# A two-layer chain of convolution and low-rank feed-forward: 7-product form one pair earlier, weight sums on GpSimd

## The chip, the core and the metric

The kernel runs on one core of a Trainium2 chip. A core has TensorE (PE in the profile; matmuls, which it writes to PSUM banks of 128 x 512 numbers), VectorE (DVE), ScalarE (ACT), GpSimd (POOL), and the queues that start DMA transfers (here those of SyncE, SP, and of ScalarE). Each engine works through its own list of instructions in order and waits on semaphores for the others. The metric is the device time of one launch in microseconds.

## What is computed

Two layers, each of them a mixing step over channels and a feed-forward step with low-rank experts, on x of 32 x 64 x 1024 numbers in float32:

```python
# layer 0: grouped convolution (9 taps, 4 groups) plus a row made from cond_128
h = conv(x, L0_cond_weight) + (c @ c_weight.T)[:, :, None] + bias[None, :, None]
out = h @ W.T + b                               # 1024 x 1024
scores = h @ gate_w.T + gate_b                  # 4 ranks, the best one is taken
final = (h @ A[:r].T @ B[:, :r].T) * weight     # r of the chosen rank, 8 to 64
x = x + out + final
# layer 1: per-sample 64 x 64 channel mix, then the same with 8 experts of rank 16
h = einsum('boi,bih->boh', agg_w, x) + agg_b[:, :, None]
out = h @ W_base.T + b_base
weights = sparsemax(h @ W_router.T)
x = x + out + einsum('bser,bse,ero->bso', einsum('bsd,edr->bser', h, A1), weights, B1)
```

## The kernel before, in words

**Tiles and pairs.** 2048 rows make 16 tiles of 128 rows a layer. Two tiles make a pair; pairs 0 to 7 are layer 0, pairs 8 to 15 layer 1. For each pair TensorE makes the mixed input of the *next* pair (`conv_half`, `mix_half`; tiles t1+2 and t2+2) between the matmuls of this pair, VectorE adds the row to it (`sum_mix`, into `mixed`), and the result is split into a high part and a rest (`split_a`: ScalarE copies to `a_hi` in a reduced format, VectorE subtracts to get `a_lo`). A product of two matrices then takes three matmuls: high x high, high x rest, rest x high. Weights are split the same way.

**Two ways to multiply.** `FULL` pairs go by `dense0`: eight blocks of 128 of the contraction, and for each of them 3 output parts x 3 matmuls. The pairs after them go by a Strassen-like form: the two tiles of a pair and the two halves of the contraction are four operands A11, A12, A21, A22 and the 432 left and right output columns are the halves of the result, so that seven products P1 to P7 (`product_a`, `product_s`) take the place of eight. The columns that are left (`PLAIN`) go by `plain`. The seven-product form needs four sums of weight blocks, called T1 to T4, and four sums of input blocks, S1 to S4.

- T sums, layer 0: `t_sums(kc)` for kc = 0 to 3, four subtractions of 128 x 432 each, in place in `w_raw`; they make T1, T3, T2, T4 in that order. `split_t(i, kc)` splits them: ScalarE into `wb_hi`, VectorE into `wb_lo`. T3 lies in the slot of the weight block B12, so its split waits for the last matmul that reads B12 (`b12_read`).
- S sums: four operations of 128 x 512 on `mixed`. GpSimd makes them (`sums(g)`) for all pairs but the first that needs them; there VectorE does (`first_sums`). `split_s` splits them; `s_hi` and `s_lo` lie on the memory of `w_raw`.

**The gate.** For each tile `gate0(T)` reads the product's extra columns from the bank b_p, on VectorE: a chain of short instructions with one exponential on ScalarE in its middle (`gate_exp`), then four writes to `u_sb`, each to both halves of its columns. TensorE transposes `u_sb` into the bank `b_u` (`turn_u`), and `split_ut` splits the result into `ut_hi` and `ut_lo`. `lora` and `rank0` multiply these by the low-rank weights and add them to the results in the banks.

**Order.** It is written out by hand in each engine's list. Before the loop over g, the lists hold pair 0 and pair 1 in full (on TensorE: `dense0` of tile 0, `second_tile(0)`, `dense0` of tile 2, `second_tile(1)`). The loop runs from g = FULL to 15: `plain` of both tiles, P1, half a mix, transpose of tile t1, P2, half a mix, transpose of t2, P4, P5, `lora` of t1, half a mix, P6, half a mix, `lora` of t2, P7, P3, `lora`. VectorE's list in the loop: gate of t1, splits of S2 and S4, gate of t2, and then `take_first`, the sums of the mix, `split_ut`, `split_a`, and the additions to the rows `xs` in turn. Where TensorE waits for others in it is in the `wait_ge` lines: P4 waits for `tlo_done[T4]`, P5 for S1 and for `sum_mix(2g+2, 1)` (both write or read the bank b_y), `lora` for `utlo_done`, `plain` of tile t2 for `finq[1]`, the last addition of the pair before it.

**Where GpSimd stands.** After its constants it waits for the splits of T2 and T4, clears `kernels_sb`, and from then on makes S sums and, in pairs 3 to 6, the T sums of layer 1 (`prep`).

## Time and profile before

| | |
|---|---|
| three runs | 505.94, 506.79 (median), 506.85 us |
| the profiled execution | 505.61 us |
| its span, first to last instruction | 503.9 us |
| TensorE's granted clock over the span | 1.00 of 2.4 GHz |
| busy: TensorE, VectorE, ScalarE, GpSimd | 499.1, 347.9, 130.4, 142.0 us |

All times of the trace count from the start of the span. Idle time of an engine is written behind its row in square brackets, with what ended it. An instruction of VectorE begins a little before the one ahead of it has ended, so the distance of two starts is shorter than a duration.

### The profile page before, as it was taken

What the parts mean: (1) busy time and instruction counts of PE and PEld (TensorE: products, weight loads), DVE (VectorE), ACT (ScalarE), POOL (GpSimd) and SP (SyncE); (2) the same over time, 40 slices, a digit from 0 to 9 for tenths busy, and PEclk for the clock granted to TensorE, in tenths of its full rate; (3) what the DMA queues carried; (4) which work ended last, traced back from release to release, by engine and by line L of the source; (5) the groups of instructions that cost most, each with busy time, mean ns of one, the idle gap of its engine ahead of it and who ended that gap; (6) DMA issues with size and microseconds to landing.
All of it is one profiled execution on the core that took longest, in us unless ns stands there. A gap on an engine that the chain in (4) does not pass through costs nothing.

```text
span 503.9 us, 8309 instructions
## 1 busy us (share of the span) xinstructions
PE 499.1 (99%) x2981; PEld 467.7 (93%) x2981; DVE 347.9 (69%) x824; ACT 130.4 (26%) x272; POOL 142.0 (28%) x122
## 2 busy tenths in 40 slices
PE   8999999999999999999999999999999999999997
PEld 8999999999999999999999899999999999999986
DVE  3966988857766685776897975665747566574753
ACT  4732334212233122331252321210212111111200
POOL 1000010003443142431205462441516244152620
PEclk9999999999999999999999999999999999999999
DMA  8845204428476574657899752433425233340212
GB/s 317 320 144 166 91 1 148 157 89 262 163 245 195 196 231 171 197 184 268 273 410 339 298 168 87 145 102 126 130 69 161 85 129 103 134 138 19 103 47 84
DMA packets 41125, 84.34 MB, mean 167 GB/s; under 512 B 3803, under 2 KB 24667, under 8 KB 41084
## 3 DMA queue, kind: packets, MB, share of 16 engines
q1 hardware_dynamic: 31884, 61.16, 36.6%
q10 hardware_dynamic: 9200, 22.65, 12.3%
q8 instruction: 24, 0.39, 0.3%
q14 instruction: 17, 0.14, 0.1%
HBM read 58.82 MB, written 24.97 MB: 166 GB/s over the span
## 4 chain that ended last, share of the span: by engine, by line
PE 98%; DMA 1%; DVE 1%; issue 0%; ACT 0%; DVEq 0%
PE b_p L1265 10%; PE b_x L1283 7%; PE b_x L1286 7%; PE b_x L1285 7%; PE b_m L1231 6%; PE b_p L1266 5%; PE b_y L1285 5%; PE b_y L1286 5%; PE b_y L1283 5%; PE b_m L1241 3%; PE b_w L1283 2%; PE b_z L1285 2%; PE b_w L1285 2%; PE b_z L1286 2%; PE b_z L1283 2%; PE b_w L1286 2%
## 5 line engine op out<-in xcount | busy, mean ns | idle before, releaser
L566 ACT CAST a_hi<-mixed 128x512 fp32r<-128x512 f32 x63 | 38.1, 620 | 167.4 <-DVE mixed L870 88.3
L1265 PE MATMUL b_p<-wp,a_hi 128*128 128x464 f32 (+1 forms) x224 | 72.5, 377 | 0.0
L512 POOL TENSOR_TENSOR xs<-xs,mixw_sb 128x464 f32<-128x464 f32 (+1 forms) x28 | 36.3, 1307 | 115.2 <-DMA xs<-x_scratch 81.5
L1266 PE MATMUL b_p<-wp,a_lo 128*128 128x232 f32 (+1 forms) x224 | 60.0, 268 | 0.0
L882 DVE TENSOR_TENSOR s_lo<-mixed,s_hi 128x512 fp32r<-128x512 f32 x56 | 45.4, 834 | 20.5 <-ACT s_hi L578 20.5
L578 ACT CAST s_hi<-mixed 128x512 fp32r<-128x512 f32 x56 | 34.7, 621 | 77.3 <-POOL mixed L484 41.2
L875 DVE TENSOR_TENSOR a_lo<-mixed,a_hi 128x512 fp32r<-128x512 f32 x63 | 47.4, 779 | 9.4 <-ACT a_hi L566 8.8
L484 POOL TENSOR_TENSOR mixed<-mixed 128x512 f32<-128x512 f32 x13 | 17.6, 1353 | 120.9 <-DVE a_lo L875 120.9
L976 DVE TENSOR_TENSOR xs<-b_x,xs 128x464 f32<-128x464 f32 (+1 forms) x54 | 33.5, 620 | 22.9 <-PE b_x L1286 20.0
L1265 PEld LDWEIGHTS b_p<-wp,a_hi 128*128 128x128 f32 x224 | 42.0, 188 | 4.7
L1266 PEld LDWEIGHTS b_p<-wp,a_lo 128*128 128x128 f32 x224 | 42.7, 191 | 0.2
L1283 PE MATMUL b_y<-wb_hi,s_hi 128*128 128x464 f32 (+1 forms) x112 | 41.2, 368 | 0.0
L1285 PE MATMUL b_y<-wb_lo,s_hi 128*128 128x464 f32 (+1 forms) x112 | 41.1, 367 | 0.0
L1286 PE MATMUL b_y<-wb_hi,s_lo 128*128 128x464 f32 (+1 forms) x112 | 41.1, 367 | 0.0
L1231 PE MATMUL b_m<-first_in,blk 128*128 128x128 f32 x256 | 32.0, 278 | 0.2 <-DMA blk<-in_xblk 0.2
L976 DVE TENSOR_TENSOR xs<-b_y,xs 128x432 f32<-128x432 f32 (+1 forms) x28 | 17.4, 620 | 20.8 <-PE b_y L1286 20.0
L1231 PEld LDWEIGHTS b_m<-first_in,blk 128*128 128x128 f32 x256 | 30.8, 194 | 0.7 <-DMA blk<-in_xblk 0.5
L1283 PE MATMUL b_x<-wb_hi,s_hi 128*128 128x432 f32 (+1 forms) x80 | 30.5, 381 | 0.0
L1286 PE MATMUL b_x<-wb_hi,s_lo 128*128 128x432 f32 (+1 forms) x80 | 29.2, 365 | 0.0
L1285 PE MATMUL b_x<-wb_lo,s_hi 128*128 128x432 f32 (+1 forms) x80 | 29.2, 365 | 0.0
L1283 PEld LDWEIGHTS b_y<-wb_hi,s_hi 128*128 128x128 f32 x112 | 21.0, 188 | 2.0
L1286 PEld LDWEIGHTS b_y<-wb_hi,s_lo 128*128 128x128 f32 x112 | 21.0, 188 | 1.9
(260 smaller groups left out, 1210.0 us busy)
## 6 DMA issues: line engine op xcount, KB each, us to landing
blk<-x_scratch SPq DMA_DIRECT2D x16, 512.0 KB, 3.3
blk<-in_xblk SPq DMA_DIRECT2D x14, 516.0 KB, 3.9
xs<-in_x SPq DMA_DIRECT2D x16, 296.0 KB, 3.6
x_scratch<-xs SPq DMA_DIRECT2D x16, 296.0 KB, 4.5
w_raw<-in_wcat SPq DMA_DIRECT2D x8, 546.0 KB, 8.3
xs<-x_scratch SPq DMA_DIRECT2D x14, 280.0 KB, 3.2
out_dram<-xs SPq DMA_DIRECT2D x14, 280.0 KB, 2.5
praw<-in_wcat ACTq DMA_DIRECT2D x8, 464.0 KB, 6.1
```

The source lines that it names most:

```text
L512: pool.tensor_tensor(x_rows, x_rows, bbase[:, a:b], ALU.add).then_inc(x_biased[q], 1)
L566: act.copy(a_hi[:, op, :, :], mixed[:, op, :, :]).then_inc(ahi_done[op], 1)
L578: act.copy(s_hi[:, i, :, :], mixed[:, S_AT[i], :, :]).then_inc(shi_done[i], 1)
L875: dve.tensor_tensor(a_lo[:, op, :, :], mixed[:, op, :, :], hi(a_hi[:, op, :, :]), ALU.subtract).then_inc(alo_done[op], 1)
L882: dve.tensor_tensor(s_lo[:, i, :, :], mixed[:, S_AT[i], :, :], hi(s_hi[:, i, :, :]), ALU.subtract).then_inc(slo_done[i], 1)
L976: dve.tensor_tensor(x_rows, src[:, 0:HALF[l]], x_rows, ALU.add).then_inc(done, 1)
L1231: ins = pe.matmul(dst, blk[s][:, at + side:at + side + QB], taps, start=(side == 0), stop=(side == 1))
L1265: pe.matmul(both, x_hi, wp[:, k, :, 0:PLAIN[l]], start=(k == 0), stop=False, skip_group_check=True)
L1266: ins = pe.matmul(dst, x_lo, wp_hi[:, k, 0:PLAIN[l]], start=False, stop=(k == NCH - 1), skip_group_check=True)
L1283: pe.matmul(dst, x_hi[:, k, :], w_hi[:, k, :], start=(first and k == 0), stop=False, skip_group_check=not first)
L1285: pe.matmul(dst, x_hi[:, k, :], w_lo[:, k, :], start=False, stop=False, skip_group_check=not first)
L1286: ins = pe.matmul(dst, x_lo[:, k, :], w_hi[:, k, :], start=False, stop=(k == HK - 1), skip_group_check=not first)
```

## The change

- `FULL` is 1: pair 1 (tiles 2 and 3) goes by the seven products. Its entries in the lists ahead of the loop are gone, and the loop begins at g = 1.
- The T sums (16 subtractions) are made by GpSimd, not by VectorE, once `a_lo` of A22 of pair 0 is made; behind them GpSimd makes the S sums of pair 1 (`sums(FULL)`), which makes `first_sums` of VectorE disappear.
- The 32 splits of T (16 on ScalarE, 16 on VectorE) stand in other places: those of T1, T4 and half of T2 within pair 0, those of T3 and the rest of T2 in pair 1.
- For tiles 2 to 15 (`together`), the gate writes its result once, for the two tiles of a pair side by side, and one transpose turns both (`turn_pair`, behind the second half mix); `split_ut` then works on 64 partitions of the bank instead of 128.

```diff
-FULL = 2
+FULL = 1
...
+        def together(T):
+            return 2 * FULL <= T < TILES
...
+            pool.wait_ge(alo_done[A22], 1)
+            for kc in range(HK):
+                t_sums(kc)
+            sums(FULL)
...
-                    for t in (T1, T2, T3, T4):
+                    for t in (T1, T3):
                         act.wait_ge(tlo_done[t], HK)
...
+                if together(T):
+                    rows_ = turned_rows(s)
+                    act.copy(ut_hi[rows_, s, :], b_u[rows_, 0:P]).then_inc(uthi_done, 1)
+                    act.copy(ut_lo[0:RANK, s, :], b_u[rows_, 0:P]).then_inc(uthi_second, 1)
+                    return
...
@@ vector, pair 0 @@
+            split_t(T1, 0)
+            split_t(T4, 0)
             dve.wait_ge(att_t, 1)
...
             finish(0, 0)
+            split_t(T1, 1)
             dve.wait_ge(aggb_mm, 1)
             dve.tensor_copy(aggb_sb[:, :], b_m[0:NB, 2 * P:2 * P + CH]).then_inc(aggb_copied, 1)
+            split_t(T4, 1)
+            split_t(T2, 0)
+            split_t(T2, 1)
             gate0(1)
             sum_mix(2, 0)
+            split_t(T1, 2)
             sum_mix(2, 1)
+            split_t(T4, 2)
             split_a(A11, 1)
...
             finish(1, 0)
-            t_sums(0)
-            t_sums(1)
...
@@ vector, loop @@
+                if g == FULL:
+                    split_t(T1, 3)
+                    split_t(T4, 3)
                 gate(2 * g + 1)
                 if g == FULL:
-                    split_ut(2 * g)
-                    for i in S_ORDER:
+                    for kc in range(HK):
+                        split_t(T3, kc)
+                    for i in (S2, S4, S1):
                         split_s(i, g)
...
+                if together(2 * g):
+                    split_ut(2 * g)
                 split_ut(2 * g + 1)
+                if g == FULL:
+                    split_t(T2, 2)
+                    split_t(T2, 3)
+                    split_s(S3, g)
...
@@ tensor @@
-            pe.wait_ge(sum_done, 7)
-            pe.wait_ge(finq[0], 1)
-            for k in range(NCH):
-                dense0(2, k)
-            pe.wait_ge(sum_done, 8)
-            second_tile(1)
...
-                turn_u(t1)
+                if not together(t1):
+                    turn_u(t1)
...
-                    turn_u(t2)
+                    if together(t1):
+                        turn_pair(g)
+                    else:
+                        turn_u(t2)
```

Three places in the lists. VectorE in pair 0, from the addition of the left columns of tile 0 (`xs0<-b_p0`) to the first instructions of the gate of tile 1, before:

```order
L991 TENSOR_TENSOR xs0<-b_p0,xs0 128x160
L1088 COPY aggb_sb<-b_m 32x64
L921 TENSOR_TENSOR sc<-b_p1,first_in 128x4
L922 SCALAR_TENSOR_TENSOR pm<-sc 128x4
L923 TENSOR_SCALAR st<-pm 128x1
```

and in the changed kernel (`wb_lo<-w_raw,wb_hi` is a split of a T sum):

```order
L1015 TENSOR_TENSOR xs0<-b_p0,xs0 128x160
L830 TENSOR_TENSOR wb_lo<-w_raw,wb_hi 128x432
L1115 COPY aggb_sb<-b_m 32x64
L830 TENSOR_TENSOR wb_lo<-w_raw,wb_hi 128x432 x3
L941 TENSOR_TENSOR sc<-b_p1,first_in 128x4
L942 SCALAR_TENSOR_TENSOR pm<-sc 128x4
L943 TENSOR_SCALAR st<-pm 128x1
```

Four splits have moved ahead of the gate of tile 1.

GpSimd from its last constant on, before:

```order
L477 MEMSET ut_lo 1x256
L517 MEMSET kernels_sb 128x2048
L484 TENSOR_TENSOR mixed<-mixed 128x512
L487 TENSOR_TENSOR mixed<-mixed 128x512
```

and in the changed kernel, the last of four equal groups of T sums and what follows:

```order
L525 TENSOR_TENSOR w_raw<-w_raw 128x432
L526 TENSOR_TENSOR w_raw<-w_raw 128x432
L528 TENSOR_TENSOR w_raw<-w_raw 128x432
L530 TENSOR_TENSOR w_raw<-w_raw 128x432
L492 TENSOR_TENSOR mixed<-mixed 128x512
L495 TENSOR_TENSOR mixed<-mixed 128x512
L497 TENSOR_TENSOR mixed<-mixed 128x512
L500 TENSOR_TENSOR mixed<-mixed 128x512
L539 MEMSET kernels_sb 128x2048
```

Sixteen T sums and four S sums now stand ahead of the clearing of `kernels_sb`.

VectorE in the changed kernel, pair 1, from the end of the gate of tile 3 to the second half of the next mix (in the list before, pair 2 had one `ut_hi` row, four `s_lo`, `xs0` and the two sums here):

```order
L953 TENSOR_SCALAR u_sb<-hid_sb,kw 128x32
L830 TENSOR_TENSOR wb_lo<-w_raw,wb_hi 128x432 x4
L895 TENSOR_TENSOR s_lo<-mixed,s_hi 128x512 x3
L1000 TENSOR_TENSOR xs0<-b_x,xs0 128x432
L880 TENSOR_TENSOR mixed<-b_m,ctx_row 128x8x64
L880 TENSOR_TENSOR mixed<-b_y,ctx_row 128x8x64
L888 TENSOR_TENSOR a_lo<-mixed,a_hi 128x512 x2
L905 TENSOR_TENSOR ut_hi<-b_u,ut_hi 64x128 x2
```

The four splits of T3 stand ahead of the splits of S, and both `ut_hi` rows of the pair behind `a_lo`.

## Rows read from the trace of the kernel before

**Rows 1.** The page: engines; chain that ended last; a ScalarE group.
```profile
PE 499.1 (99%) x2981; PEld 467.7 (93%) x2981; DVE 347.9 (69%) x824; ACT 130.4 (26%) x272; POOL 142.0 (28%) x122
...
PE 98%; DMA 1%; DVE 1%; issue 0%; ACT 0%; DVEq 0%
...
L578 ACT CAST s_hi<-mixed 128x512 fp32r<-128x512 f32 x56 | 34.7, 621 | 77.3 <-POOL mixed L484 41.2
```
**Rows 2.** Timeline of TensorE (start, duration, what): starts of pairs 1 to 4, P5.
```profile
48.56 0.31 PE L1364 MATMUL b_p<-wp,a_hi 128*128 128x228 f32 x1
...
82.13 0.41 PE L1265 MATMUL b_p<-wp,a_hi 128*128 128x456 f32 x1
...
114.97 0.37 PE L1265 MATMUL b_p<-wp,a_hi 128*128 128x456 f32 x1
...
130.89 0.36 PE L1283 MATMUL b_y<-wb_hi,s_hi 128*128 128x432 f32 x1
...
145.98 0.37 PE L1265 MATMUL b_p<-wp,a_hi 128*128 128x456 f32 x1
```
**Rows 3.** Timeline of GpSimd, then of VectorE, around the start of pair 3.
```profile
113.83 1.29 POOL L487 TENSOR_TENSOR mixed<-mixed 128x512 f32<-128x512 f32 x1
115.19 1.62 POOL L489 TENSOR_TENSOR mixed<-mixed 128x512 f32<-128x512 f32 x1
116.96 1.56 POOL L492 TENSOR_TENSOR mixed<-mixed 128x512 f32<-128x512 f32 x1
...
114.37 1.29 DVE L882 TENSOR_TENSOR s_lo<-mixed,s_hi 128x512 fp32r<-128x512 f32 x1 [1.61 <-ACT s_hi L578]
...
118.05 0.49 DVE L921 TENSOR_TENSOR sc<-hid_sb,first_in 128x4 f32<-128x4 f32 x1
```
**Rows 4.** The same two engines within pair 3.
```profile
129.90 1.20 POOL L502 TENSOR_TENSOR praw<-praw 128x464 f32<-128x464 f32 x1
131.18 1.53 POOL L504 TENSOR_TENSOR praw<-praw 128x464 f32<-128x464 f32 x1
...
130.11 3.13 DVE L875 TENSOR_TENSOR a_lo<-mixed,a_hi 128x512 fp32r<-128x512 f32 x2 [0.69 <-ACT a_hi L566]
```
**Rows 5.** Timeline of VectorE: pair 0, and four splits of T3.
```profile
23.37 1.27 DVE L875 TENSOR_TENSOR a_lo<-mixed,a_hi 128x512 fp32r<-128x512 f32 x2
...
36.09 0.61 DVE L976 TENSOR_TENSOR xs<-b_x,xs 128x432 f32<-128x432 f32 x1 [0.67 <-PE b_x L1313]
...
38.44 0.21 DVE L1088 COPY aggb_sb<-b_m 32x64 f32<-32x64 f32 x1 [1.00 <-PE b_m L1431]
39.76 0.16 DVE L921 TENSOR_TENSOR sc<-b_p,first_in 128x4 f32<-128x4 f32 x1 [1.10 <-PE b_p L1376]
...
42.33 0.68 DVE L867 TENSOR_TENSOR mixed<-b_m,ctx_row 128x512 f32<-128x512 f32 x1
43.83 0.69 DVE L867 TENSOR_TENSOR mixed<-b_x,ctx_row 128x512 f32<-128x512 f32 x1 [0.81 <-PE b_x L1231]
...
47.13 0.29 DVE L890 TENSOR_TENSOR ut_hi<-b_u,ut_hi 64x128 fp32r<-64x128 f32 x1
...
51.13 0.32 DVE L991 TENSOR_TENSOR xs<-b_p,xs 128x160 f32<-128x160 f32 x1
...
69.45 2.17 DVE L798 TENSOR_TENSOR wb_lo<-w_raw,wb_hi 128x432 fp32r<-128x432 f32 x4
```
**Rows 6.** Timeline of TensorE: first low-rank matmul of tiles 0, 1 and 6.
```profile
35.49 0.36 PE L1311 MATMUL b_x<-lb,ut_hi 128*128 128x432 f32 x1
...
47.48 0.46 PE L1311 MATMUL b_z<-lb,ut_hi 128*128 128x432 f32 x1
...
133.25 0.36 PE L1311 MATMUL b_z<-lb,ut_hi 128*128 128x432 f32 x1
```
**Rows 7.** Timeline of TensorE: half a convolution early and later.
```profile
4.61 2.46 PE L1231 MATMUL b_m<-first_in,blk 128*128 128x128 f32 x16 [0.20 <-DMA blk<-in_xblk]
...
45.42 1.95 PE L1231 MATMUL b_m<-first_in,blk 128*128 128x128 f32 x16
```

More of the change, by code:

```diff
@@ L694, in _ @@
             split_ut(1)
+            act.wait_ge(b12_read, 1)
+            split_t(T3, 0)
+            split_t(T3, 1)
             split_a(A21, 1)
             split_a(A22, 1)
-            for kc in (0, 1):
-                for i in (T1, T2, T4):
-                    split_t(i, kc)
-            gate_exp(2)
-            for kc in (2, 3):
-                for i in (T1, T2, T4):
-                    split_t(i, kc)
-            split_ut(2)
-            act.wait_ge(b12_read, 1)
-            for kc in range(HK):
-                split_t(T3, kc)
-            gate_exp(3)
-            split_a(A11, 2)
-            split_a(A12, 2)
-            split_ut(3)
-            split_a(A21, 2)
-            split_a(A22, 2)
-            for i in S_ORDER:
-                split_s(i, FULL)
+            split_t(T1, 3)
+            split_t(T4, 3)
             for g in range(FULL, LAST + 1):
@@ L721, in _ @@
                 gate_exp(2 * g)
+                if g == FULL:
+                    split_t(T3, 2)
+                    split_t(T3, 3)
                 if g > FULL:
@@ L739, in _ @@
                     load_slot(T3, P7)
-                split_ut(2 * g)
+                if g == FULL:
+                    split_t(T2, 2)
+                    split_t(T2, 3)
+                    for i in (S2, S4, S1, S3):
+                        split_s(i, g)
+                if not together(2 * g):
+                    split_ut(2 * g)
                 if g < LAST:
@@ L751, in _ @@
                     split_a(A12, g + 1)
+                if together(2 * g):
+                    split_ut(2 * g)
                 split_ut(2 * g + 1)
@@ L888, in split_ut @@
                 dve.wait_ge(uthi_done, T + 1)
-                if T < TILES:
+                if together(T):
+                    rows_ = turned_rows(s)
+                    dve.wait_ge(uthi_second, T + 1)
+                    dve.tensor_tensor(ut_hi[turned_rows(1 - s), s, :], b_u[rows_, 0:P], hi(ut_hi[rows_, s, :]),
+                                      ALU.subtract).then_inc(utlo_done, 1)
+                elif T < TILES:
                     dve.tensor_tensor(ut_hi[RANK:P, s, :], src[RANK:P, :], hi(ut_hi[RANK:P, s, :]),
@@ L918, in gate0 @@
                 hid = hidden(T)
-                if T > 1:
+                if together(T):
+                    dve.wait_ge(ut_done, T - s)
+                elif T > 1:
                     dve.wait_ge(ut_done, T - 1)
@@ L1099, in _ @@
             finish(1, 0)
-            t_sums(0)
-            t_sums(1)
-            for i in (T1, T2, T4):
-                split_t(i, 0)
-            t_sums(2)
-            for i in (T1, T2, T4):
-                split_t(i, 1)
-            gate0(2)
-            t_sums(3)
-            for kc in (2, 3):
-                for i in (T1, T2, T4):
-                    split_t(i, kc)
-            split_ut(2)
-            for kc in range(HK):
-                split_t(T3, kc)
-            finish(0, 1)
-            gate0(3)
-            sum_mix(4, 0)
-            sum_mix(4, 1)
-            split_a(A11, 2)
-            split_a(A12, 2)
-            split_ut(3)
-            sum_mix(5, 0)
-            sum_mix(5, 1)
-            take_plain(1, 1)
-            finish_first(1, 1)
-            split_a(A21, 2)
-            split_a(A22, 2)
-            first_sums()
-            finish_second(1, 1)
             def take_first(g):
@@ L1140, in _ @@
                     split_s(S4, g)
+                if g == FULL:
+                    split_t(T1, 3)
+                    split_t(T4, 3)
                 gate(2 * g + 1)
                 if g == FULL:
-                    split_ut(2 * g)
-                    for i in S_ORDER:
+                    for kc in range(HK):
+                        split_t(T3, kc)
+                    for i in (S2, S4, S1):
                         split_s(i, g)
@@ L1147, in _ @@
                     take_first(g)
-                if g == PAIRS - 1:
-                    split_ut(2 * g)
                 if g < LAST:
                     sum_mix(2 * g + 2, 0)
-                if g not in (FULL, PAIRS - 1):
+                if not together(2 * g):
                     split_ut(2 * g)
@@ L1161, in _ @@
                     split_a(A12, g + 1)
+                if together(2 * g):
+                    split_ut(2 * g)
                 split_ut(2 * g + 1)
+                if g == FULL:
+                    split_t(T2, 2)
+                    split_t(T2, 3)
+                    split_s(S3, g)
                 if PREP_FIRST <= g <= PREP_LAST:
```

47 lines of the change are left out of this document (30 added, 17 removed).

## Prediction

> **What bounds the kernel now.** I read three views: the page (engines and chain), TensorE's timeline at the borders of the pairs, and the timelines of VectorE and GpSimd side by side. TensorE is busy 499.1 us of a span of 503.9 and makes up 98% of the chain that ended last [rows 1]. So work taken from TensorE comes straight off the time, as long as its operands are there when it comes to them; work on the others costs nothing until it makes TensorE wait. TensorE's timeline gives the price of a pair: pair 1, in full, lasts from 48.56 to 82.13, 33.57 us; pair 3, by seven products, from 114.97 to 145.98, 31.01 us [rows 2]. (Pair 2 holds other work too and is no measure.) The question is then whether VectorE, ScalarE and GpSimd deliver what pair 1 needs 34 us earlier than now.
>
> **Taken from TensorE.** Pair 1 by seven products: 33.57 - 31.01 = 2.56 us. One transpose less in each of seven pairs: it is 128 columns wide like one of the 16 steps of half a convolution, which take 1.95 us, some 0.11 each [rows 7]; since TensorE overlaps neighbours I take half of that, 0.05 us each, between 0 and 0.11: 0.35 us. Together 2.9 us.
>
> **What GpSimd and VectorE do to each other.** This decides the case. At 114.37 VectorE begins a subtraction of 128x512 from two operands in SBUF while GpSimd is in a sum that ends at 113.83 + 1.29 = 115.12. It ends at 115.66, that is 0.54 us after GpSimd's end, with 1.29 us in place of the 0.64 of an undisturbed one, two of which take 1.27 [rows 3, 5]. GpSimd's next sum takes 1.62 in place of 1.29. So the one who comes second stands still until the other's instruction is over. In pair 3 the same gives two subtractions in 3.13 us [rows 4], against 1.27 undisturbed [rows 5]: 1.5 to 1.6 us each while GpSimd has a queue of sums. Even an instruction of 4 columns waits: it takes 0.49 us at 118.05 and ends with GpSimd's sum at 118.52 [rows 3]; the like one with one operand in PSUM at 39.76 takes 0.16 [rows 5]. Additions that read one operand from PSUM aren't hit.
>
> GpSimd now makes 16 sums of 128x432. None is in the trace; the 128x464 one takes 1.20 [rows 4], so 1.20 x 432/464 = 1.12 each, 18 us in all. It starts where `a_lo` of A22 ends, at 23.37 + 1.27 = 24.6 [rows 5]; alone it would be busy to 42.6, and with VectorE's instructions of about 0.4 to 0.5 between them to about 47. Over just this stretch VectorE has its new splits, each with two SBUF operands: each costs 1.12 + some 0.37 = 1.5 us instead of the 0.52 of rows 5 (four in 2.17).
>
> **Pair 0, step by step.** (a) From 24.6 to 36 VectorE has eight such instructions (two in the gate of tile 0, two that split the low-rank weights, two new splits, two that make the attention diagonal). Its idle stretches there take up the first ones. I estimate that the two new splits end near 35.7 and `ut_hi` at 36.0, where TensorE wants it at 35.49 [rows 6]: 0.5 late. The diagonals wait about 1.1 each, so the addition that starts at 36.09 starts at about 38.1. (b) The addition's group lasts to about 39.5. Then four splits at 1.5 us, 5.9: the gate of tile 1 starts at 45.3 and not at 39.76. The idle 1.00 + 1.10 us there [rows 5] would have covered four undisturbed splits to the tenth of a us; it doesn't cover 5.9. (c) The gate has two more instructions with two SBUF operands; they wait once for about 1.0: 6.4 late at the next row, 42.33. (d) Two more splits, 0.52 each if GpSimd is done by then, one of them in the idle 0.81 before 43.83 [rows 5] and the other in a wait for ScalarE: 0.4 comes back. The split `ut_hi` of tile 1 (47.13) is the last thing before TensorE's 47.48, with no slack there [rows 5, 6]. So pair 1 starts about 5.9 us late; TensorE has waited for it in the pieces that end at the low-rank matmul of tile 0, the copy of `aggb_sb`, the transpose of tile 1, the bank b_m and the low-rank matmul of tile 1. Bounds: with the part before 38 at nothing and no wait in the gate, 37.45 + 6.1 gives 3.8 late, less 0.3: 3.5. With sums of 1.25 us, each step longer: 7.7.
>
> **Pair 1.** All times here are those before plus 5.9. (e) `plain` of tile 3 wants the addition at 51.13 + 0.32 = 51.45 finished; it is due 2.55 after the pair's start, at 51.11 [rows 2, 5]. Before, nothing there waited for it. 0.35 us; between 0.2 and 0.5. (f) P5 is due 130.89 - 114.97 = 15.92 after the start of a pair [rows 2], so at 48.56 + 5.9 + 0.35 + 15.9 = 70.7. It waits for `sum_mix(4, 1)`. VectorE's list up to it: gate of tile 2 from 57.4, 2.57 us (39.76 to 42.33) [rows 5] plus 0.3 for the reduction ahead of it, plus about 2.2 for two waits, since GpSimd's four S sums (1.29 each and more) [rows 3] run from 56.1 to 61.7: 62.5. Two splits, 1.1: 63.6. Gate of tile 3, 2.9: 66.5. Four splits of T3, 2.1: 68.6. ScalarE may make `s_hi` only after these, 0.62 [rows 1]; then three `s_lo` of 0.61, `xs` 0.55, two sums of the mix 0.65 each: 72.9. P5 waits 2.2 us. Between 0.8 (no wait in the gate of tile 2) and 2.9. P4, and the transpose of the pair, are due at 68.3 and have what they need. P6 and P7 need T2, S3 by 75 and later: no wait.
>
> **Later pairs.** (g) `split_ut` of the first tile has moved behind `a_lo`. In pair 3, `a_lo` ends at 130.11 + 3.13 = 133.24 and TensorE wants `ut_hi` at 133.25 [rows 4, 6]: 0.3 us late, in this pair alone, since GpSimd's sums came later there than in pairs 4 to 6. Otherwise nothing: the S sums of pair 2 on GpSimd have the place that they have in pair 3 now. The removed `first_sums` and 16 T sums shorten VectorE's list by some 11 us, all of it beside TensorE's work, worth nothing.
>
> **Sum.** 5.9 + 0.35 + 2.2 + 0.3 - 2.9 = +5.8 us on a span of 503.9: 509.7, and with the 1.7 us around it 511.4. The profiled execution (505.61) lies 1.2 below the median of the runs; on the median, 506.79 + 5.8 = **512.6 us**, slower by 1.1%. Ends of the terms: 3.5 + 0.2 + 0.8 - 2.9 = +1.6 and 7.7 + 0.5 + 2.9 + 0.3 - 2.9 = +8.5, so 508.4 to 515.3.
>
> **Rivals.** *Faster:* the two engines don't hold each other up here, or GpSimd's sums find gaps between VectorE's instructions. Then (b) leaves 0.4 late, (e) 0.35, (f) nothing: 0.75 + 0.3 - 2.9 = -1.9, 504.9 us. For it: the four splits then fit the idle 2.1 us; against it: rows 3 and 4, with the same kind of instruction. It decides when a split in pair 0 takes under about 0.9 us. *Short instructions slip through:* full-size ones wait, those of the gate don't. Then the gate terms of (c) and (f) and part of (a) go: some 3.5 late in pair 0, 0.8 at P5: 508.5 us. Against it: the row at 118.05. The Trainium skill ("SBUF — State Buffer", section "Who interferes with whom") says that issue order, not an instruction's shape, decides who blocks; by that this rival is out, and the trace agrees with the 0.49 us of a 4-column row. *Slower still:* TensorE waits some 6 us in pieces within 22 us, and its granted clock, 1.00 throughout now, may fall from 2.4 to 1.2 GHz for a while. At the start half a convolution takes 2.46 us against 1.95 [rows 7], part of it at the lower level; if 3 us of work ran at that level, they would take 6: 515.6 us. The Trainium skill ("TensorE: Matmul & The Clock Gate", section "What's actually happening") has an idle TensorE fall back to the lower level; the trace has no wait long enough to show it. That the change doesn't do what it says can be excluded: the lists show the seven products of pair 1.
>
> **How the numbers follow.** Forecast 512.6 with 0.63; clock 0.06; short instructions slip through 0.12; faster 0.13; and 0.06 for a mixture of small waits that ends near zero. The range leaves out the faster case and half of the last: 507.5 to 516.5. A measurement of this kernel tells about 0.2%, 1 us, from no change. Faster by more than that 0.13, within it 0.06, slower 0.81.
>
> **What would show it.** In the profile of the changed kernel: GpSimd busy from 24.6 to about 47 with 16 sums, many of 1.4 to 1.6 us; splits of T by VectorE of 1.5 us each between 39 and 46; idle TensorE before the transpose of tile 1 and its low-rank matmul, about 4.5 us together, released by VectorE; pair 1 beginning near 54.5 and lasting 33.5 us, with 2 us of wait before P5; pairs 2 and later each shorter by 0.05. I am wrong if the splits there take 0.6, if the gate's 4-column instructions stay at 0.16, or if TensorE's waits are all under 0.5.

## The result, and the profile after

The changed kernel takes 515.15 us (median of six executions, 512.92 to 519.69) where the kernel before, measured beside it, takes 506.58 (505.48 to 508.54): a ratio of 1.0195, 95% interval 1.0168 to 1.0221. It is slower, by 8.6 us between the medians and by 9.4 us between the profiled executions (515.03 and 505.61). The forecast was 512.6, +5.8 us.

The page of the changed kernel: its engines, and the chain that ended last.

```profile
PE 501.0 (98%) x2946; PEld 467.3 (91%) x2946; DVE 353.3 (69%) x816; ACT 133.0 (26%) x276; POOL 174.7 (34%) x146
...
PE 82%; DVE 8%; DMA 5%; issue 1%; ACT 1%; ACTq 0%; SPq 0%; DVEq 0%
```

Against [rows 1], TensorE makes 35 matmuls fewer and is yet 1.9 us longer busy, GpSimd has 32.7 us more, and of the chain 8% is now VectorE and 5% DMA, which had 1% each. The waits of TensorE in the same profile (line waited for, releaser, us in total, times, longest) give the places:

```profile
PE b_m L1424 <- DVE att_rep L1083: 2.2, 1, 2.2
PE b_y L1293 <- DVE mixed L880: 2.2, 1, 2.2
PE b_z L1328 <- DVE ut_hi L908: 2.0, 1, 2.0
```

They are the attention's transpose, P5 of pair 1, and the low-rank matmul of tile 1. TensorE's timeline (start, duration, what, idle before it) shows what they do to the stages, to be held against [rows 2, 6]:

```profile
36.44 0.21 PE L1424 MATMUL b_m<-ident,att_rep 32*128 32x32 f32 x1 [2.24 <-DVE att_rep L1083]
...
39.10 0.56 PE L1328 MATMUL b_x<-lb,ut_hi 128*128 128x432 f32 x1
...
54.56 0.46 PE L1328 MATMUL b_z<-lb,ut_hi 128*128 128x432 f32 x1 [1.97 <-DVE ut_hi L908]
...
55.64 0.41 PE L1275 MATMUL b_p<-wp,a_hi 128*128 128x456 f32 x1
...
74.26 0.44 PE L1293 MATMUL b_y<-wb_hi,s_hi 128*128 128x432 f32 x1 [2.19 <-DVE mixed L880]
...
90.96 0.37 PE L1275 MATMUL b_p<-wp,a_hi 128*128 128x456 f32 x1
```

Pair 1 starts at 55.64 instead of 48.56, 7.1 us late. Of this, 0.5 us was there before any sum: the first product begins at 11.76 instead of 11.27, because the first half convolution, which runs partly at the lower level of the clock, took 2.98 us instead of 2.46 [rows 7]. It took 2.05 to 3.33 us in the profiled executions of this study, so this is no price of the sums. Pair 1 lasts 35.32 us instead of 33.57. At pair 2 the kernel is 8.8 us behind (90.96 against 82.13), and of the 9.4 us only 0.6 come later: pairs 2 to 6 take 157.0 us where they took 156.9, pair 7 27.8 against 27.4, pair 8 30.2 against 30.1.

Part of the 35.32 is the clock. These stretches of TensorE (from:to, length, busy and instructions, granted clock, DMA share, GB/s) lie at and behind the first two waits:

```profile
34.00:37.20 3.20, 0.96 (x7) 1.00 0.62 196
37.20:40.70 3.50, 3.50 (x14) 0.51 0.36 128
40.70:44.20 3.50, 3.50 (x23) 1.00 0.40 152
71.00:74.80 3.80, 1.61 (x9) 1.00 0.33 127
74.80:78.30 3.50, 3.50 (x12) 0.51 0.00 0
```

After standing still for 2.2 us TensorE resumed, and a moment later was granted 1.2 GHz in place of 2.4 for some 3.4 us, twice. Behind the third wait, 1.97 us, the level stayed at 1.00. The 12 matmuls of P5 took 3.99 us, from the start of the first to that of the next step (74.26 to 78.25), most of it at the lower level, against 2.36 in pair 4, so the second fall cost 1.6 us. The forecast sum had nothing for it.

What VectorE did in the gate of tile 0 and behind it (same columns):

```profile
25.76 0.66 DVE L942 TENSOR_TENSOR_SCAN pm<-sc 128x4 f32<-128x4 f32 x1
26.46 0.15 DVE L943 TENSOR_SCALAR st<-pm 128x1 f32<-128x1 f32 x1
26.53 0.98 DVE L944 TENSOR_SCALAR keep<-pm 128x3 f32<-128x3 f32 x1
...
27.94 0.75 DVE L948 TENSOR_TENSOR st<-st 128x1 f32<-128x1 f32 x1
28.73 1.16 DVE L949 TENSOR_SCALAR kw<-keep,st 128x4 f32<-128x4 f32 x1
29.92 0.73 DVE L956 TENSOR_SCALAR u_sb<-b_p,kw 128x16 f32<-128x16 f32 x4
...
35.28 1.02 DVE L1083 TENSOR_SCALAR att_rep<-att,stat 32x128 f32<-32x128 f32 x1
...
40.06 0.61 DVE L1000 TENSOR_TENSOR xs<-b_x,xs 128x432 f32<-128x432 f32 x1 [0.47 <-PE b_x L1330]
...
42.91 3.69 DVE L830 TENSOR_TENSOR wb_lo<-w_raw,wb_hi 128x432 fp32r<-128x432 f32 x3
46.52 0.15 DVE L941 TENSOR_TENSOR sc<-b_p,first_in 128x4 f32<-128x4 f32 x1
...
49.80 0.68 DVE L880 TENSOR_TENSOR mixed<-b_m,ctx_row 128x512 f32<-128x512 f32 x1
...
60.21 1.27 DVE L944 TENSOR_SCALAR keep<-pm 128x3 f32<-128x3 f32 x1
```

and three of GpSimd's sums, the first, a long one of the sixteen, and the first of the S sums:

```profile
25.29 1.12 POOL L525 TENSOR_TENSOR w_raw<-w_raw 128x432 f32<-128x432 f32 x1 [21.79 <-DVE a_lo L888]
...
30.89 2.12 POOL L526 TENSOR_TENSOR w_raw<-w_raw 128x432 f32<-128x432 f32 x1
...
57.35 1.29 POOL L492 TENSOR_TENSOR mixed<-mixed 128x512 f32<-128x512 f32 x1 [9.80 <-DVE a_lo L888]
```

Instructions of one to four columns take 0.66 to 1.27 us; alone, they take 0.16 to 0.23. They end with GpSimd's sums: the scan at 26.42, `keep` at 27.51, `st` at 28.69 and `kw` at 29.89, where the first four sums end at 26.41, 27.48, 28.67 and 29.86. In between, rows of one column with one operand (0.15) and rows that read PSUM went through. It goes both ways: the sum of 2.12 us began while VectorE was in a subtraction with two operands in SBUF and ended 1.0 us after that one.

### The profile page after: what moved, and what is told of

The parts are those of the page before. It is cut to its first block, busy times and chain, and to the rows that moved or that the text cites. A ratio compares the mean times of both kernels' runs of the same rounds, so it can differ in the third digit from the quotient of the medians.

```text
span 513.3 us, 8290 instructions
## 1 busy us (share of the span) xinstructions
PE 501.0 (98%) x2946; PEld 467.3 (91%) x2946; DVE 353.3 (69%) x816; ACT 133.0 (26%) x276; POOL 174.7 (34%) x146
## 4 chain that ended last, share of the span: by engine, by line
PE 82%; DVE 8%; DMA 5%; issue 1%; ACT 1%; ACTq 0%; SPq 0%; DVEq 0%
PE b_p L1275 9%; PE b_x L1293 7%; PE b_x L1296 6%; PE b_x L1295 6%; PE b_m L1241 4%; PE b_y L1293 4%; PE b_y L1296 4%; PE b_y L1295 4%; PE b_p L1276 4%; PE b_m L1251 3%; DMA x_scratch<-xs 2%; PE b_z L1295 2%; PE b_z L1293 2%; PE b_z L1296 2%; PE b_w L1293 2%; PE b_w L1295 2%
## 5 line engine op out<-in xcount | busy, mean ns | idle before, releaser
L1275 PE MATMUL b_p<-wp,a_hi 128*128 128x464 f32 (+1 forms) x240 | 77.8, 377 | 0.1
L895 DVE TENSOR_TENSOR s_lo<-mixed,s_hi 128x512 fp32r<-128x512 f32 x60 | 48.8, 835 | 23.8 <-ACT s_hi L600 23.8
L1276 PE MATMUL b_p<-wp,a_lo 128*128 128x232 f32 (+1 forms) x240 | 64.3, 268 | 0.0
L1000 DVE TENSOR_TENSOR xs<-b_x,xs 128x432 f32<-128x432 f32 (+1 forms) x57 | 35.3, 619 | 21.7 <-PE b_x L1296 19.1
L1275 PEld LDWEIGHTS b_p<-wp,a_hi 128*128 128x128 f32 x240 | 45.0, 188 | 5.4 <-DVE xs L1015 0.4
L1293 PE MATMUL b_y<-wb_hi,s_hi 128*128 128x464 f32 (+1 forms) x120 | 44.7, 373 | 2.2 <-DVE mixed L880 2.2
L1276 PEld LDWEIGHTS b_p<-wp,a_lo 128*128 128x128 f32 x240 | 45.8, 191 | 0.2
L1295 PE MATMUL b_y<-wb_lo,s_hi 128*128 128x464 f32 (+1 forms) x120 | 44.6, 372 | 0.0
L1296 PE MATMUL b_y<-wb_hi,s_lo 128*128 128x464 f32 (+1 forms) x120 | 44.6, 372 | 0.0
L1293 PE MATMUL b_x<-wb_hi,s_hi 128*128 128x432 f32 (+1 forms) x88 | 33.5, 381 | 0.3 <-DVE xs L1000 0.3
```

The costliest lines, as they stand in the source:

```text
L895: dve.tensor_tensor(s_lo[:, i, :, :], mixed[:, S_AT[i], :, :], hi(s_hi[:, i, :, :]), ALU.subtract).then_inc(slo_done[i], 1)
L1000: dve.tensor_tensor(x_rows, src[:, 0:HALF[l]], x_rows, ALU.add).then_inc(done, 1)
L1275: pe.matmul(both, x_hi, wp[:, k, :, 0:PLAIN[l]], start=(k == 0), stop=False, skip_group_check=True)
L1276: ins = pe.matmul(dst, x_lo, wp_hi[:, k, 0:PLAIN[l]], start=False, stop=(k == NCH - 1), skip_group_check=True)
L1293: pe.matmul(dst, x_hi[:, k, :], w_hi[:, k, :], start=(first and k == 0), stop=False, skip_group_check=not first)
L1295: pe.matmul(dst, x_hi[:, k, :], w_lo[:, k, :], start=False, stop=False, skip_group_check=not first)
```

## Is it the two engines, or the new lists?

The theory: GpSimd and VectorE hold each other up. The rival: the new order of VectorE's and ScalarE's lists costs the time. Two kernels keep all waits and signals and cut GpSimd's sums to two columns, all twenty or only the sixteen of the weights.

```diff
-pool.tensor_tensor(raw_block(kc, 0), raw_block(kc, 1), raw_block(kc, 0), ALU.subtract)
+pool.tensor_tensor(raw_block(kc, 0)[:, 0:2], raw_block(kc, 1)[:, 0:2], raw_block(kc, 0)[:, 0:2], ALU.subtract)
...
-pool.tensor_tensor(mixed[:, A22, :, :], mixed[:, A21, :, :], mixed[:, A22, :, :], ALU.add)
+pool.tensor_tensor(mixed[:, A22, :, 0:c], mixed[:, A21, :, 0:c], mixed[:, A22, :, 0:c], ALU.add)
```

> The changed kernel with the twenty sums that GpSimd makes up to P5 cut to 2 columns of each block, so that their waits and signals stay and their transfer of data goes; left out of the computation: the rest of those sums, the slots hold raw weights there. Theory 1, GpSimd and VectorE hold each other up: VectorE's rows in the two gates and the splits go back to the times of the kernel before, the attention's transpose starts at 33.6 and not 36.44, pair 1 at 49 to 50 and not 55.64, P5 waits under 0.5 us, TensorE is granted its high level throughout, and the time is 504 to 506.5. Theory 2, the new order of VectorE's and ScalarE's lists is what costs: pair 1 still starts after 54 and the time stays within 1.5 us of 515. The difference between 515.15 and this run prices all of GpSimd's work.

> Only the sixteen weight sums (25.3 to 47.6) cut to 2 columns, the four sums of the mixed operands (57.4 to 62.9) in full; left out of the computation: the rest of the sixteen. If the waits before pair 1 come from the sixteen alone, pair 1 starts at 49 to 50 and the first fall of the clock is gone. The gate of tile 2 still takes 5.3 us beside the four sums and P5 still waits about 2 us with a fall of the clock after it: 507 to 508.5. If P5's wait was only inherited from the late start, it is gone here too and the time is that of the run with both cut, within 0.5 us.

With all twenty cut: 504.79 us (503.85 to 509.27, ten executions), ratio 0.9991 (0.9963 to 1.0019). TensorE, then VectorE's gate of tile 0, in that kernel (its lines are one further down):

```profile
48.85 0.41 PE L1276 MATMUL b_p<-wp,a_hi 128*128 128x456 f32 x1
...
65.19 0.36 PE L1294 MATMUL b_y<-wb_hi,s_hi 128*128 128x432 f32 x1
...
80.27 0.37 PE L1276 MATMUL b_p<-wp,a_hi 128*128 128x456 f32 x1
```

```profile
25.59 0.17 DVE L943 TENSOR_TENSOR_SCAN pm<-sc 128x4 f32<-128x4 f32 x1
...
25.86 0.22 DVE L945 TENSOR_SCALAR keep<-pm 128x3 f32<-128x3 f32 x1
```

The same lists, in the same order, without GpSimd's traffic: pair 1 at 48.85, no wait at P5, pair 1 in 31.42 us, the clock high throughout. So the lists cost about 0.5 us, in pair 1 (31.42 against 30.91 for a pair that waits for nothing), and the full sums cost 515.15 - 504.79 = 10.4 us. Cutting a sum also makes its result ready sooner, but that is not what was gained: in the changed kernel neither VectorE nor ScalarE waits for a result of GpSimd before the sums of pair 2 (the first such wait ends at 89.57), so it is the hold-up. With the sixteen alone cut, 509.13 us (506.20 to 511.60; ratio 1.0049, 1.0022 to 1.0077): pair 1 starts at 49.10, but the gate of tile 2 takes as long as in the changed kernel, P5 waits 2.14, the clock falls behind it, and pair 1 takes 35.32 us again. So the sixteen cost 6.5 us, all ahead of pair 1, and the four S sums 3.9 (35.32 - 31.42), the wait at P5 and the lower clock behind it. Both parts of the theory stand; its estimate for this run, 507 to 508.5, was too low. In the profiled execution a load came late in pair 7 (below).

## Can the sums be moved out of the way?

If the 2.2 us at the attention's transpose come from sums beside the gate of tile 0, starting them later frees it:

```diff
             pool.wait_ge(alo_done[A22], 1)
+            pool.wait_ge(att_op, 5)
...
-            split_t(T1, 0); split_t(T4, 0)    (ahead of split_ut(0))
+            split_t(T1, 0); split_t(T4, 0)    (behind split_ut(0) on ScalarE, behind finish(0, 0) on VectorE)
```

> GpSimd starts its sixteen sums only when the attention's last step is done (about 6 us later), and the splits T1,0 and T4,0 stand behind tile 0's transposed rows on VectorE and ScalarE, all else as in the changed kernel. Theory, the 2.2 us at the attention's transpose come from GpSimd's sums beside the gate of tile 0: the transpose starts at 33.6, the low-rank product of tile 0 at 35.5 to 36, and the clock's first fall (1.7 us) goes; but the sums now run to about 54 and lie over all of gate tile 1, so that pair 1 starts only 1.5 to 3.5 us earlier than 55.64. Time 510 to 513. Rival, the sums cost the same wherever they lie and their delay holds up splits and gate of tile 1 as long as was gained: 514.5 to 516.

517.42 us (516.86 to 521.10), ratio 1.0240 (1.0202 to 1.0278): the rival, and dearer than it said. The transpose did go back to 33.74 and the first low-rank matmul to 35.59, so the cause of that wait is shown. But two groups of three splits then took 4.09 and 4.15 us (1.63 for three with the sums cut), TensorE waited 2.4 us for `aggb_sb`, the gate of tile 1 stood behind all of it and was itself held up by the sums, and pair 1 began at 58.44. The same test for the S sums lets them start only behind the gate of tile 2:

```diff
+            pool.wait_ge(gated, 4 * (2 * FULL + 1))
             sums(FULL)
```

> The changed kernel, but GpSimd begins its four S sums only when the gate of tile 2 is done, so that they run beside the splits T1,3 and T4,3 and the gate of tile 3. Theory, what is lost is a wait for each instruction that finds GpSimd at work, so long instructions and chains of short ones pay alike: the gate of tile 2 goes from 5.3 to 2.9 us, the two splits and the gate of tile 3 become longer by about 3 to 4 waits of 0.5 to 1.1, P5 waits 1.5 to 3 us and pair 2 starts within 1 us of 90.96. Rival, only the gate of tile 2 was hit hard and the sums would have run free of harm beside the splits: P5 waits under 0.7 us, no second fall of the clock, pair 2 starts before 88.5 and the time is under 512.5.

517.61 us (516.24 to 521.90), ratio 1.0232 (1.0184 to 1.0281). The gate of tile 2 was done in 2.9 us as expected, and the gate of tile 3, 2.9 in the changed kernel, then took 5.9: P5 waited 2.63, pair 2 began at 91.23 against 90.96. The hold-up moved one gate on, at the same price. That fits the theory that what is lost is a wait for each instruction that meets a sum, wherever it meets it.

The last placement is back on VectorE, at four places of its list:

```diff
+            t_sums(0)
             dve.wait_ge(mlp_mm, 3)
...
+            t_sums(1)
             finish(0, 0)
...
             gate0(1)
+            t_sums(2)
             sum_mix(2, 0)
...
             sum_mix(3, 1)
+            t_sums(3)
...
             finish(1, 0)
+            first_sums()
```

> The changed kernel with all twenty sums back on VectorE (the four of block column 0 behind the gate of tile 0, of 1 ahead of the additions of tile 0, of 2 behind the gate of tile 1, of 3 behind the last mix of tile 3, the four S sums ahead of the gate of tile 2). VectorE's instructions keep their undisturbed times (0.15 to 0.23 in the gates, 0.60 a split) but it has 16 sums of some 0.55 and 4 of 0.65 more, 11 us; about 9.5 us of idle pieces lie between 24 and 60 us, few of them whole. Theory, GpSimd's help is worth little because each of its sums takes about 0.4 us from VectorE before pair 1 and 0.7 in the gate of tile 2: this kernel is within 2.5 us of the changed one, 513 to 517.5. Rival, the hold-up is dearer than the sums themselves: below 512.

517.98 us (515.29 to 520.57), ratio 1.0208 (1.0161 to 1.0254). The time lies just above the theory's range, but the sums did not put it there: in the profiled execution pair 1 starts at 52.64, three us earlier than in the changed kernel, and pair 2 too.

```profile
52.64 0.41 PE L1284 MATMUL b_p<-wp,a_hi 128*128 128x456 f32 x1
...
87.81 0.37 PE L1284 MATMUL b_p<-wp,a_hi 128*128 128x456 f32 x1
```

Not all of this is the sums' price. VectorE has made only twelve of its sixteen weight sums when pair 1 starts; the last four (52.15 to 54.43) and the S sums come after it, and P5 comes 19.99 us into the pair instead of 18.62. P5 starts at 72.64 against 74.26: up to there all twenty sums are 1.6 us cheaper on VectorE, at 0.60 us for each weight sum, than standing still for GpSimd's. The rest of the 3.2 us at pair 2 is the clock: P5 waited 2.14 us here and the granted clock did not fall behind it. The advantage is lost in pair 7, where TensorE waits 4.0 and 1.6 us for additions and then works at the lower clock. The chain of waits of this kernel names what the additions wait for, a store of x and the load behind it (start, us, what):

```profile
250.87 7.62 DMA x_scratch<-xs
...
258.93 11.34 DMA xs<-in_x
```

## What the fall of the clock costs

Fourteen matmuls of 80 columns, into columns of a bank that nothing reads, fill TensorE's two waits:

```diff
+            def fill(count):
+                for _ in range(count):
+                    pe.matmul(b_w[:, HALF[0]:512], ones[:, :], ones[:, 0:512 - HALF[0]], start=False, stop=False, ...)
...
+                    fill(14)     (ahead of the attention's transpose)
...
+                    fill(14)     (ahead of P5 of pair 1)
```

> The changed kernel with 14 small matmuls (80 columns, into columns of a bank that nothing reads) ahead of each of TensorE's two waits of 2.2 us, the attention's transpose and P5: nothing becomes ready sooner, but TensorE is idle for some 0.4 us instead of 2.2. Theory, the clock falls after these two waits because TensorE stands still in them: the granted clock is the high level throughout, all starts up to 36.44 and 74.26 stay, and the time is 3.4 us shorter, 511 to 512.3. Rival, the clock falls for another reason (the stage at 37 or P5 itself): both falls stay and so does the time, 514.5 to 515.5.

The same two stretches, then TensorE's timeline (the profile has two records for each of these matmuls, 28 for 14):

```profile
37.20:40.70 3.50, 3.50 (x23) 1.00 0.35 129
74.80:78.30 3.50, 3.50 (x23) 1.00 0.00 0
```

```profile
72.15 3.25 PE L1360 MATMUL b_w<-ones 128*128 128x80 f32 x28
75.20 0.45 PE L1293 MATMUL b_y<-wb_hi,s_hi 128*128 128x432 f32 x1
...
90.37 0.37 PE L1275 MATMUL b_p<-wp,a_hi 128*128 128x456 f32 x1
```

The granted clock stayed at 1.00 in both stretches that had 0.51. Of the four executions two have a mean of 1.000 and two 0.997, one fall, which in the profiled one comes in pair 7; of the six of the changed kernel, five have two falls or more. So the falls go with the standing still. It does not bring one each time: with the sums on VectorE the wait of 2.14 us before P5 was followed by none, while in the changed kernel with a later load (below) one of 1.97 us was, and one of 1.55 was not. The time did not follow: 516.85 us (515.39 to 518.28), ratio 1.0213 (1.0186 to 1.0241). Three things took the gain. I had sized the filler wrongly: it took 3.1 us and not 1.9, so the transpose came at 37.16 (0.7 late) and P5 at 75.20 (0.9 late). The first fall was worth at most some 0.5 us: although the low-rank matmul of tile 0 and those around it ran faster, TensorE then waited 1.1 us for the gate of tile 1, and pair 1 began at 55.88, 0.2 late where the transpose had been 0.7 late. The second was worth 1.5 us, about what was read above: from P5's start to the end of the pair 15.2 us instead of 16.7. Pair 2 began at 90.37, 0.6 earlier in spite of the 0.9; in the profiled execution pair 3 (32.08 us against 31.02) and above all pair 7 (31.60 against 27.84) lost it again. A lower clock costs only where TensorE is what the next stage waits for.

## What makes a small VectorE instruction wait

My forecast counted instructions with two operands in SBUF. `keep` and `att_rep` have one and a scalar. Two kernels put probes of four columns or one into the stretch of the sixteen sums; their results are not used. Each was executed once (528.75 and 528.91 us), and only its rows are read.

> The changed kernel with eight rounds of four small instructions more on VectorE (4 columns each, results not used) just before the split T1,0 at 36.2, where GpSimd is in its sums: a TENSOR_SCALAR with a constant, a TENSOR_SCALAR with its scalar in SBUF, a COPY, a TENSOR_TENSOR of two operands in SBUF. In the changed kernel's trace the gate's rows with a scalar from SBUF and its scan took 0.66 to 1.27 and those with one operand 0.15 to 0.16. Theory, an instruction waits for GpSimd when it reads two operands in SBUF, and a scalar that lies in SBUF counts as one: the second and fourth kind show 0.4 to 1.3 while GpSimd is at work, the first and third 0.14 to 0.16. Rival, every TENSOR_SCALAR and COPY from SBUF to SBUF waits, by its mode: the first and third are hit as well. Rival 2, only TENSOR_TENSOR waits, and the rows of the gate were long for another reason: the second kind stays at 0.2.

Here the first TENSOR_SCALAR with a constant took 1.09 us, the ones with a scalar in SBUF 1.06 to 1.16 in all six cases in which GpSimd was at work, one TENSOR_TENSOR 1.06, and COPY always 0.15, but only since GpSimd's short gaps opened just when it came. That left open whether COPY goes free, so the second probe moves each kind into the middle of a sum:

> The second probe of VectorE, in the same place as the first, since there all but one of the first and third kind fell into GpSimd's short gaps. Eight tests, and ahead of each a TENSOR_TENSOR of two SBUF operands (which ends when a sum of GpSimd ends) and four RECIPROCALs of one column, which move the tested instruction some 0.3 us into GpSimd's next sum: TENSOR_SCALAR with a constant on 4 columns, on 1 column, COPY of 4 columns, TENSOR_SCALAR with its scalar in SBUF on 1 column, TENSOR_TENSOR of 1 column, COPY of 1 column, TENSOR_SCALAR with a constant on 4 columns and on 3. Theory A, two operands in SBUF make an instruction wait, a scalar in SBUF being one: only the fourth and fifth take 0.5 to 0.9 and all others 0.15. Theory B, it is the one-input instruction's width: of four columns (or two) at a time it waits as well, on one column it does not: the first, third and seventh wait, the second, fourth and sixth take 0.15 to 0.2; the fifth waits by its two inputs. The eighth, 3 columns, tells whether an odd count escapes.

```profile
37.73 0.91 DVE L1099 TENSOR_SCALAR hid_sb<-first_in 128x4 f32<-128x4 f32 x1
...
38.87 0.13 DVE L1101 TENSOR_SCALAR hid_sb<-first_in 128x1 f32<-128x1 f32 x1
...
39.98 1.00 DVE L1103 COPY hid_sb<-first_in 128x4 f32<-128x4 f32 x1
...
41.22 0.19 DVE L1105 TENSOR_SCALAR hid_sb<-first_in,pk 128x1 f32<-128x1 f32 x1
...
42.20 0.87 DVE L1107 TENSOR_TENSOR hid_sb<-first_in 128x1 f32<-128x1 f32 x1
...
43.32 0.13 DVE L1109 COPY hid_sb<-first_in 128x1 f32<-128x1 f32 x1
...
44.42 1.00 DVE L1111 TENSOR_SCALAR hid_sb<-first_in 128x4 f32<-128x4 f32 x1
```

Theory B. TENSOR_SCALAR and COPY from SBUF to SBUF wait on four columns and pass on one; the scalar's place does not matter (0.19 with the scalar in SBUF); a TENSOR_TENSOR waits even on one. The eighth, of 3 columns, came after GpSimd's last sum and tells nothing; `keep`, of 3 columns, took 0.98 in the changed kernel, and 0.22 alone. The Trainium skill ("SBUF — State Buffer", section "Who interferes with whom") names copies and TENSOR_SCALAR in the modes that use both ports beside the instructions with two inputs in SBUF as those that contend with GpSimd; these rows agree, and add that a gate's 3 and 4 columns are enough. I had read the section for its rule on two inputs only.

## The transpose by itself, and pair 7

Only the shared transpose, in the kernel before with its two full pairs:

```diff
+        def together(T):
+            return 2 * FULL <= T < TILES          (FULL stays 2)
...
-                turn_u(t1)
+                if not together(t1): turn_u(t1)
...
-                    turn_u(t2)
+                    turn_pair(g) if together(t1) else turn_u(t2)
```

with the copies and splits of `ut_hi` and `ut_lo` as in the change.

> The kernel before, with two pairs in full and all its sums on VectorE, and only the one transpose for both tiles of a pair, from pair 2 on (six pairs), with the copies and splits that belong to it. My prediction took 0.05 us a pair and nothing else; pairs 4 and 5 of the changed kernel's trace are 0.10 shorter each. Theory: pairs 2 to 7 0.05 to 0.10 shorter each, 0.3 to 0.6 us in all, so a ratio of 0.999, 505.7 to 506.2 where the kernel before has 506.4. Rival: the splits behind a_lo come late in more than one pair and eat it: ratio 1.000 or above.

508.26 us (506.69 to 509.82, twelve executions), ratio 1.0033 (1.0013 to 1.0053): slower. Pairs 2 to 6 were 0.10 us shorter each (30.91 against 31.01), the upper end of what I had taken. Up to there the theory held; pair 7, which neither it nor the rival had in mind, took 31.72 us instead of 27.43. TensorE's wait there, and SyncE's timeline (stores of x, then the loads that wait for them), in this kernel:

```profile
PE b_x L1309 <- DVE xs L1003: 2.2, 1, 2.2
```

```profile
243.83 0.94 SPq L350 DMA_DIRECT2D x_scratch<-xs  x2
250.63 0.81 SPq L345 DMA_DIRECT2D xs<-in_x  x2
```

In the kernel before, the two stores are issued 4.4 us after the pair's start and their loads 4.6 us later; here 5.7 and 6.8. The DMA engines' share over the pair is 0.93 there and 0.94 here: the second layer's weights come in, and a load of x that other transfers delay reaches VectorE too late. Two kernels tried to mend it. The first holds the plain weights' load back until the stores have landed, once with the shared transpose and once in the changed kernel:

```diff
-                    act.wait_ge(pl_done, 2 * PAIRS)
-                    act.dma_start(wp_raw...)     (ahead of gate_exp(2 * g + 1))
+                    act.wait_ge(x_stored[3], 16 * g)
+                    act.wait_ge(x_stored[1], 16 * g)
+                    act.wait_ge(pl_done, 2 * PAIRS)
+                    act.dma_start(wp_raw...)     (behind it)
```

> The kernel before with one transpose a pair (as the run before of that kind), and in pair 7 ScalarE issues the 928 KB load of the second layer's plain weights only when the stores of x of the pair before have landed. In the run with the transposes alone pairs 2 to 6 were each 0.10 us shorter and pair 7 was 31.72 instead of 27.43: there this load was issued 0.4 us before the stores, in the kernel before 0.95 us behind the first, and the stores took 6.8 us instead of 4.6, so that the next load of x landed 2.2 us after TensorE wanted it. Theory, the order of these transfers is the cause: pair 7 goes back to 27.3 to 27.6 us, the run-to-run spread shrinks, and the time is 505.3 to 506, ratio 0.998 to 0.9995. Rival, the DMA engines are full there and any order leaves the same lateness, or the plain weights now come late for pair 8: 507 to 509.

> The changed kernel with the same delay of the load of the plain weights in pair 7, nothing else. The changed kernel's executions lie at 512.9 to 519.7, and the profiled one has two falls of the clock. Theory, what makes them lie above 515.2 is the late load of x in pair 7: the executions shrink to 512.5 to 515.5, median 514 to 514.8. Rival, they differ by the waits and the clock ahead of pair 2: spread and median stay, 515 to 516.

509.53 us (507.65 to 512.21), ratio 1.0065 (1.0041 to 1.0089), and 517.26 (516.57 to 520.64), ratio 1.0230 (1.0199 to 1.0262). Both lie above all that was expected. Pair 7 took 33.61 and 33.66 us. In the first, the loads of x were issued at 247.99, as early as in the kernel before, and nothing waited for them; the chain of waits shows what came instead:

```profile
248.00 9.69 DMA wp_place<-in_wcat
...
258.70 0.90 DVE wp L851
...
260.90 1.13 DVE xs L1004 x2
...
262.07 2.08 PE b_z L1268 x8
```

The load held back took 9.7 us, and its split stands on VectorE's list ahead of the additions that free a bank of TensorE's: 3.3 us of wait. So the order of the transfers does decide which of them is late, which is the first half of the theory, but the 4 us that I took from one were missing at the next; the remedy, and with it the forecast of the time, fell. The other kernel keeps pair 7 as it was and shares the transpose in pairs 2 to 6 only:

```diff
-            return 2 * FULL <= T < TILES
+            return 2 * FULL <= T < TILES - 2
```

> The kernel before with one transpose a pair in pairs 2 to 6 only; pair 7, where the second layer's weights are loaded, keeps its two transposes and its order of copies and splits. Theory, it is the new order within pair 7 that shifts its transfers against each other: pairs 2 to 6 stay 0.10 us shorter each, pair 7 goes back from 31.7 to some 27.4 us, and the time is 505.6 to 506.0 where the kernel before has 506.2 (ratio 0.998 to 0.9998); that version would be ahead of both kernels. Rival, the lateness hangs on when pair 7's transfers meet each other and not on its own lists, and any shift ahead of it can bring it: pair 7 takes 30 to 32 us in most executions and the time is 507.5 to 509.

506.35 us (505.43 to 509.41, twelve executions), ratio 1.0014 (0.9990 to 1.0037): between the two. Seven executions lie at 505.4 to 506.4, about where the theory has them, and five at 507.6 to 509.4, where the rival has them. In the profiled one pair 7 took 27.77 us, although its loads of x went out 12.5 us after the pair's start, as late as with the transpose shared there too (and 8.9 in the kernel before). So pair 7's own lists do matter, since with them changed the lowest of twelve was 506.69, and yet the lateness comes in some executions without them. What decides it stays open. The profiled execution of the changed kernel itself had no such wait in pair 7, but TensorE waited there 2.4 to 4.0 us for an addition in those of most of its variants. This is also the likely reason, not shown, why executions of one kernel differ: the two of the changed kernel above 518 us have a mean granted clock of 0.990 and 0.986, where two falls give 0.993. No kernel of this study is ahead of the kernel before by more than its measurement tells.

## Why the prediction came out as it did

The forecast held its direction and range (507.5 to 516.5) and named the mechanism, and GpSimd's sixteen sums ran from 25.29 to 47.56, as it said (24.6 to about 47). The start of pair 1 was met within 1.2 us by some luck: (a) was too small by 2.0 us and (b) too large by 1.4. By its own letters, in the profiled execution:

- **(a)** mis-sized. The addition of tile 0 came at 40.06, 4.0 late, not 2.0; 0.5 of the 4.0 is the late start of the first product. Of the gate of tile 0 I had counted two instructions; four waited (`pm`, `keep`, `st`, `kw`), 2.4 us in all, and `att_rep`, which I had not counted, 0.7; the two splits of the low-rank weights, which I had, took 3.5 us instead of 2.5. So the attention's transpose, where I saw no wait, cost TensorE 2.24 us. The probes show why: width counts, not only the number of operands.
- **(b)** smaller: the four splits from 41.5 to 46.6 took 0.76, 0.81, 1.53 and 1.50 us, 4.5 without their overlap and not 5.9; the gate of tile 1 came at 46.52 against 45.3 forecast. About 1.2 of the surplus of (a) was left.
- **(c), (d)** right: 0.7 more in the gate (forecast 1.0), 0.4 given back. Pair 1 began 7.1 late (6.6 without the late start), forecast 5.9, bounds 3.5 and 7.7. The waits lay elsewhere than I said: 2.24 us at the attention's transpose and 1.97 at the low-rank matmul of tile 1, but 0.13 at the transpose of tile 1.
- **(e)** right: `plain` took 5.53 us against 5.09 in pair 4, 0.44 for 0.35.
- **(f)** right in size and cause: 2.2 forecast, 2.19 measured; the run with the sixteen sums cut shows that it is the four S sums' doing. The sum below has 2.4: P5 came 18.62 us after the start of its pair, where pair 4 has 15.83, and 0.4 of the 2.8 is (e).
- **(g)** smaller: pair 3 of the changed kernel lost 0.1 us, not 0.3; but pair 6 lost 0.5 (31.43 against 30.91), which I had not seen. With five transposes less, pairs 2 to 6 come to +0.1.
- **Taken from TensorE**: 2.66 for pair 1 (33.57 - 30.91), and 0.10 for each transpose where I took 0.05.
- **Missing from the sum**: 1.6 us for P5 at the lower clock, and 0.5 in pairs 7 and 8.

Together 7.1 + 0.4 + 2.4 + 1.6 - 2.7 + 0.1 + 0.5 = 9.4 us.

Of the rivals, *Faster* (no mutual hold-up) is refuted by the runs with the sums cut. Its price, 504.9, is near that of the kernel without them, 504.79, whose ratio is known to 0.3%. *Short instructions slip through* is refuted by the rows of the gates and the probes, but for one-operand instructions of one column, which do pass; its terms also add up to 508.8 and not 508.5 (3.5 + 0.35 + 0.8 + 0.3 - 2.9 = +2.05). *Slower still* came true beside the forecast and not in place of it, at half its price. I gave it 0.06 and said that the trace had no wait long enough to show it, and had not held my own 2.2 us at P5 against it. The Trainium skill ("TensorE: Matmul & The Clock Gate", section "What's actually happening") has activity release a throttle that is the default; this trace agrees as far as it goes, with two waits of 2.2 us followed by 1.2 GHz, and the filled waits without. In the run with the sixteen sums cut, two of six executions were granted the high level throughout, and the changed kernel's fastest, 512.92 us, was as well: a wait of this length may but need not bring a fall. That execution, without the missing term, lies 0.3 us from the forecast.

## What to carry to other kernels

Before work moves to GpSimd, list what VectorE does in the same stretch and count every instruction that reads two operands in SBUF or copies or scales more than one column from SBUF to SBUF: each that meets a sum costs up to the rest of that sum, and a gate's chain of small ones pays most. Here 16 sums of 1.1 us on GpSimd cost TensorE 6.5 us, and with all twenty sums on VectorE, at 0.6 us for each of the sixteen, P5 of pair 1 came 1.6 us earlier. Where a stage's wait for an operand reaches some 2 us, price the work behind it at both levels of the clock, but only on the path.

## What the runs showed of the hardware

- Inside a GpSimd sum, VectorE's TENSOR_SCALAR and COPY from SBUF to SBUF took 0.91 to 1.00 us at 4 columns (0.16 alone) and passed at 1 (0.13, or 0.19 with the scalar in SBUF); a TENSOR_TENSOR of 1 column took 0.87; RECIPROCAL of 1 column (0.14), TENSOR_REDUCE of 8 (0.15), MAX8 of 8 (0.17) and TENSOR_SCALAR of 16 to 64 columns read from PSUM (0.23 to 0.28) passed.
- The scan, with both its operands in SBUF, waits like a TENSOR_TENSOR (0.66 to 1.18 us for 4 columns, 0.17 alone).
- Waits of 2.24 and 2.19 us were each followed by some 3.4 us at 1.2 GHz; P5 took 3.99 us in place of 2.36. The two waits filled with matmuls kept 2.4 GHz. One wait of 2.14 us brought no fall.
- With the DMA engines 93% busy through pair 7, new lists there went with a load of x for which TensorE waited 2.2 us, and holding a 928 KB load back by some 4 us made that one late instead (9.7 us to landing, 3.3 us of wait).
